# A post-norm decoder on one core: the row of maxima sent from ScalarE's DMA queue, and new due times for two phases

## The reference, cut to what matters

```python
# layer 0; layer 1 is the same without the bias, its q, k and v go through a width of 64
q, k, v = heads(x @ Wq), heads(x @ Wk), heads(x @ Wv)          # (16, 16 heads, 512, 16)
logits = einsum('bhqd,bhkd->bhqk', q, k) / 4 + fourier_bias     # bias(h, i - j)
attn = softmax(where(causal, logits, -inf))
x = layernorm(x + einsum('bhqk,bhkd->bhqd', attn, v) @ Wo)
# layer 0 goes on: cross-attention to 64 context rows, then ten gated experts of width 128 (top 2 of 8, 2 shared)
# layer 1 goes on: cross-attention to the same context, then a feed-forward of width 1024 with a sine in it
```

## Time and profile before

| | us |
|---|---|
| median of 3 runs (lowest, highest) | 4129.87 (4127.6, 4133.61) |
| the profiled execution: its own time | 4140.3 |
| its span from first to last instruction | 4138.5 |
| phase 1: first piece to last | 64 to 1540 |
| phase 2 | 1577 to 3359 |
| phase 3 | 3370 to 4138 |

### The profile page before, as it was taken

One profiled execution on the slowest core, in us unless ns is written; L12 is line 12 of the kernel. 1 busy time (PEld: TensorE's weight loads), 2 busy tenths in 40 slices (PEclk: granted clock), 3 DMA queues, 4 the chain that ended last, 5 costly groups with the idle time before them and its releaser, 6 DMA issues. The chain is left out here.

```text
span 4138.5 us, 59033 instructions
## 1 busy us (share of the span) xinstructions
PE 3415.8 (83%) x19630; PEld 2589.5 (63%) x19630; DVE 2920.1 (71%) x8450; ACT 1999.0 (48%) x3687; POOL 1285.3 (31%) x1713
## 2 busy tenths in 40 slices
PE   3888898888888845799999999999998756888886
PEld 2566666666666534567777777777776535666664
DVE  5578787777787743566666666766665436999996
ACT  3455555555555522244444444444444334666564
POOL 1134333343333431122222222222222102444443
PEclk8899999899999967999999999999999767999998
DMA  7444434444344112244444444444443320000000
GB/s 180 73 83 74 79 70 95 78 79 76 69 98 74 26 36 65 59 74 84 83 83 83 83 83 83 85 85 84 83 86 69 70 74 1 27 25 31 21 26 16
DMA packets 207788, 284.55 MB, mean 69 GB/s; under 512 B 50880, under 2 KB 136128, under 8 KB 198784
## 3 DMA queue, kind: packets, MB, share of 16 engines
q1 hardware_dynamic: 207488, 280.78, 34.1%
HBM read 179.75 MB, written 96.73 MB: 67 GB/s over the span
## 5 line engine op out<-in xcount | busy, mean ns | idle before, releaser
L1308 DVE CUSTOM_DVE_ANT_0 ps<-ps,future 128x512 f32<-128x512 f32 (+3 forms) x2048 | 958.0, 513 | 337.1 <-PE ps L942 330.0
L1629 ACT ACTIVATE pt<-ps 128x512 f32<-128x512 f32 x1280 | 720.3, 597 | 512.8 <-PE ps L963 499.8
L963 PE MATMUL ps<-q_stack,k_stack 97*128 97x512 f32 (+3 forms) x2048 | 566.5, 356 | 211.0 <-DMA q_stack<-nmaxT 179.0
L1812 POOL TENSOR_SCALAR_AFFINE_SELECT pt<-pt 128x256 f32<-128x256 f32 x1024 | 401.1, 429 | 738.0 <-ACT pt L1629 737.6
L942 PE MATMUL ps<-k_stack,q_stack 96*128 96x512 f32 (+3 forms) x2048 | 543.5, 350 | 52.8 <-DVE nmax L1308 33.6
L963 PEld LDWEIGHTS ps<-q_stack,k_stack 97*128 97x128 f32 x2048 | 367.4, 200 | 349.0 <-DMA q_stack<-nmaxT 212.2
L942 PEld LDWEIGHTS ps<-k_stack,q_stack 96*128 96x128 f32 x2048 | 378.1, 205 | 130.2 <-issue 44.2
L1834 POOL TENSOR_TENSOR hid<-hid,gate_of 128x512 f32<-128x512 f32 x128 | 164.3, 1283 | 690.7 <-DVE hid L1448 690.7
L977 PE MATMUL ps<-pt,v_ones 128*32 128x512 f32 (+3 forms) x4096 | 335.1, 472 | 31.9 <-POOL pt L1812 31.8
L816 PE MATMUL ps<-eh,w_hi 128*128 128x512 f32 (+1 forms) x672 | 281.5, 419 | 13.9 <-DVE xl L1289 11.4
L1308 DVE DVE_READ_ACCUMULATOR2_ANT nmax<- 128x1 f32 x2048 | 285.7, 139 | 0.3
(11 more groups left out here) (272 smaller groups left out, 8122.7 us busy)
## 6 DMA issues: line engine op xcount, KB each, us to landing
qk_scratch<-parts SPq DMA_DIRECT2D x64, 1024.0 KB, 5.8
q_stack<-qk_scratch SPq DMA_DIRECT2D x384, 128.0 KB, 5.0
k_stack<-qk_scratch SPq DMA_DIRECT2D x384, 128.0 KB, 5.7
gate_of<-gate_scratch SPq DMA_DIRECT2D x128, 256.0 KB, 5.0
x_mid<-x_ring SPq DMA_DIRECT2D x32, 512.0 KB, 2.6
x_ring<-x_mid SPq DMA_DIRECT2D x32, 512.0 KB, 5.1
w_stage<-in_w SPq DMA_DIRECT2D x17, 512.0 KB, 10.4
x_ring<-in_x SPq DMA_DIRECT2D x16, 512.0 KB, 4.6
```

The lines of the kernel that those rows point to most:

```text
L963: done = e.matmul(bank(bank_of[piece])[:, at:at + SEQ - j * P], a.k[0:97, base + h, j * P:(j + 1) * P], a.q[0:97, base + h, j * P:SEQ], st ...
L1308: done = e.tensor_tensor_reduce(src, src, future[:, SEQ - width:SEQ], -1.0, 3e38, ALU.add, ALU.min, nmax[:, g % 2, u // 5 * 2 + h, t:t + 1])
L1629: e.activation(dst, src, ACT.Exp).then_inc(exp_up.sem)
L1812: done = e.affine_select(out=blk, in_=blk, compare_op=ALU.is_ge, fill=0.0, base=0, pattern=[[0, 2], [1, P]], channel_multiplier=-1)
```

## The change

`mr` moves from SyncE's program to ScalarE's, with the same wait and the same DMA, and the due times of phases 1 and 2 are all new. Phase 3 is untouched. The numbers of pieces stay the same.

```diff
 TABLE = {
-    1: (74.24, {
+    1: (74.79, {
         "tensor": {
...
-            "N": [10.33, 35.92, 49.97, 68.22],
-            "PV": [39.6, 50.95, 65.92, 80.92],
+            "N": [25.914, 49.331, 63.644, 80.459],
+            "PV": [54.077, 65.337, 76.55, 94.888],
...
-            "xv": [95.77],
+            "xv": [103.921],
...
         "scalar": {
...
-            "N": [10.68, 36.36, 50.32, 68.96],
+            "N": [26.78, 49.641, 63.913, 80.701],
+            "mr": [27.324, 51.039, 64.237, 81.053],
...
         "sync": {
-            "ld 1": [-78.68],
-            "send": [-42.19, -34.21],
-            "rows": [-37.05, -26.06, -11.85, 4.41],
-            "mr": [16.55, 36.73, 51.02, 69.33],
-            "st 1": [183.02],
-            "kl": [81.48],
+            "ld 1": [-84.38],
+            "send": [-25.748, -17.605],
+            "rows": [-22.895, -13.151, 1.014, 47.474],
+            "st 1": [205.092],
+            "kl": [91.368],
         },
     }),
-    2: (91.43, {
+    2: (91.03, {
...
         "scalar": {
...
+            "mr": [138.692, 161.135, 182.14, 202.403],
...
         "sync": {
...
-            "mr": [128.05, 152.69, 182.69, 201.54],
...
-        max_row = [signal(f"max_row{k}", "sync", "mr", 1, 16, lambda key, k=k: key[1] % 2 == k) for k in range(2)]
+        max_row = [signal(f"max_row{k}", "scalar", "mr", 1, 16, lambda key, k=k: key[1] % 2 == k) for k in range(2)]
...
@@ in scalar(e) @@
+                elif kind == "mr":
+                    n, g = key
+                    a = att[n // BATCH]
+                    base = (g % a.sets) * GROUP
+                    e.wait_ge(*nmax_copy[key])
+                    e.dma_start(a.q[96:97, base:base + GROUP, :].bitcast(F32).rearrange("p h (t q) -> p (h t) q", q=P),
+                                a.nmaxT[:, :].bitcast(F32)).then_inc(max_row[g % 2].sem, 16)
@@ in sync(e) @@
-                elif kind == "mr":
...
```

More of the change, by code:

```diff
@@ L127 @@
 TABLE = {
-    1: (74.24, {
+    1: (74.79, {
         "tensor": {
[21 rows of a table removed]
[23 rows of a table added]
         },
         "scalar": {
[16 rows of a table removed]
[18 rows of a table added]
         },
         "vector": {
[17 rows of a table removed]
[18 rows of a table added]
         },
         "gpsimd": {
[L190 to L195, removed]
+            "sel": [45.796, 52.932, 61.307, 63.867, 73.059, 75.047, 89.481, 93.418],
+            "ln a0": [114.094],
+            "tb x0": [122.81],
+            "xs": [135.171, 140.315, 146.923, 151.897, 158.674, 161.06, 167.095, 170.965],
+            "xe": [141.859, 143.757, 153.041, 158.142, 162.556, 165.821, 173.869, 174.921],
+            "ln x0": [194.141],
@@ L207 @@
         "tensor": {
[25 rows of a table removed]
[25 rows of a table added]
         },
         "scalar": {
[19 rows of a table removed]
[20 rows of a table added]
         },
         "vector": {
[18 rows of a table removed]
[18 rows of a table added]
         },
         "gpsimd": {
-            "tb a1": [54.64],
-            "sel": [143.18, 148.25, 164.75, 172.21, 191.62, 196.65, 209.64, 216.88],
-            "ln a1": [269.21],
-            "h2": [None, None, -37.99, -29.93, -19.31, -11.84, 0.07, 7.56, 16.45, 22.74],
-            "ln ex": [42.94],
+            "tb a1": [123.318],
+            "sel": [172.319, 185.37, 202.259, 207.051, 228.077, 232.025, 243.304, 250.411],
@@ L281 @@
+            "ln a1": [305.965],
+            "h2": [None, None, -2.365, 7.429, 15.398, 21.908, 35.083, 41.236, 50.486, 56.541],
+            "ln ex": [76.515],
         },
         "sync": {
-            "ld 2": [-87.57],
-            "send": [74.31, 94.78],
-            "rows": [104.53, 124.28, 146.7, 170.94],
-            "mr": [128.05, 152.69, 182.69, 201.54],
-            "st 2": [273.18],
-            "gh": [-48.24],
-            "sg": [-46.41, -45.9, -36.67, -28.61, -17.99, -9.09, 1.38, 8.88],
+            "ld 2": [-38.115],
@@ L290 @@
+            "send": [109.08, 138.923],
+            "rows": [141.11, 160.207, 187.217, 210.043],
+            "st 2": [307.51],
+            "gh": [-18.786],
+            "sg": [-9.841, -6.46, -0.9, 5.922, 18.591, 28.003, 36.64, 43.797],
         },
@@ L1940, in sync @@
                                             "(h d) t -> d h t", d=HDIM)).then_inc(rows_in[g % a.sets].sem, 16)
-                elif kind == "mr":
-                    n, g = key
-                    a = att[n // BATCH]
-                    base = (g % a.sets) * GROUP
-                    e.wait_ge(*nmax_copy[key])
-                    e.dma_start(a.q[96:97, base:base + GROUP, :].bitcast(F32).rearrange("p h (t q) -> p (h t) q", q=P),
-                                a.nmaxT[:, :].bitcast(F32)).then_inc(max_row[g % 2].sem, 16)
                 elif kind == "kl":
```

## The result

| | before | after |
|---|---|---|
| median of 4 runs (lowest, highest), us | 4130.17 (4127.6, 4133.61) | 4034.82 (4020.1, 4036.3) |
| ratio after / before, 95% interval | | 0.9761 [0.9737, 0.9785] |
| profiled execution: own time, span, us | 4140.3, 4138.5 | 4036.08, 4034.3 |
| phase 1, phase 2, phase 3, us | 1478.5, 1784.4, 768 | 1412.1, 1745.6, 769 |

The changed kernel is 95 us faster at the median. 180 were forecast. The time lies inside the range, which had been drawn wide enough to take in rival A, and the gain is more than twice that of rival A (36 us).

A forecast was written before the change was run, and what follows sets the result against it. TensorE was taken as the bound in phases 1 and 2, its longest wait being T's for the row of maxima. -150 - 65 + 30 + 5 = -180 us gave 3960 profiled, 3950 us at the median; range 3850 to 4095.

The forecast's parts named there:

- rival A: Landing of the row of maxima stays as long as before despite ScalarE's queue: -36 us, 4094 us; chance 0.13.
- the short landing: On ScalarE's queue a row of maxima lands in 1.8 to 2.5 us, with nothing ahead in its ring.
- Part 3: New order in phases 1 and 2: less cover costs 1.9 us a batch in phase 1, 0 in phase 2; +30 us.
- Part 1: `mr` on ScalarE's queue: 85% of T's 179 us wait for the row of maxima won, -150 us.
- Part 2: TensorE's clock partly recovers as idle time goes: 2 us a batch in phase 1, 2.1 in phase 2; -65 us.
- (a): Phase 1: xv waits for kl, 0 to 2 us, taken as 1 us.
- (b): PV.1 to PV.3 have 1.2 to 1.9 us behind the last T; PV.3 loses 0.4 of its cover.
- (c): xq.0 has 2.0 us of cover behind tc x0, before 5.5; wait of 0 to 1.5 us, taken as 0.7.
- shifts that I can't see: Unseen effects of the new order, taken as a loss of 0.8 us.
- (d): A batch of phase 1 runs some 10 us longer in the table, counted once when the last batch drains: +5 us.
- C: T.0.0 of phase 1 waits for a late mr.0 amid kl and rows.3: slower, 4213 or 4161 us; chance 0.09.
- B: VectorE or GpSimd takes over in phase 1, which gains nothing: about -80 us, 4050 us; chance 0.11.

The follow-up runs named there:

- run 4: Changed kernel with two of the six DMAs of each `rows` group, 256 KB instead of 768, all engines doing the same work: 3848.38 us, ratio 0.9296.
- run 3: Changed kernel with SyncE holding back rows.3 and rows.1 in phase 1 and rows.2 in phase 2 until a row of maxima has landed: 4010.13 us, 0.9681.
- run 8: Kernel before with two due times changed, so SyncE issues mr.2 and mr.3 of phase 1 ahead of the `rows` they followed: 4049.76 us, 0.9777.
- run 2: Kernel before, old due times, with only `mr` moved to ScalarE's program right behind each N: 4121.19 us, 0.9957.
- run 5: Changed kernel with SyncE holding back rows.3 and rows.1 until mr.0 and mr.2 have landed, in phase 1 only: 3970.25 us, 0.959.
- run 6: Run 5 plus 15 due times of phase 2 that put more work ahead of T.1.0 and T.3.0: 3918.35 us, 0.9461.
- run 10: Kernel before with the changed kernel's due times for xs, xe, xp and xo of phase 1, moved 13.54 us earlier: ratio 1.0106.
- run 7: Kernel before with xe.1, xe.3 and xe.5 put ahead of the next xs on VectorE and GpSimd: 4165.6 us, 1.0055.
- run 9: Kernel before with xs.4 to xs.7 of phase 1 put on TensorE ahead of the xp they follow: ratio 1.0102.

## Why the prediction was right or wrong, point by point

**What bounds the kernel: right.** TensorE's idle time and above all the wait of T for the row of maxima was the thing to win; run 4 took it away and phase 2 was left with 1.3 us of idle time a batch.

**The cause of the long landing: right in the bytes, wrong in the queue.** I had read that the long ones are those behind `rows`, and wrote "the bytes ahead in the ring". Runs 3, 4 and 8 show that it is the transfers under way at the issue; run 2 and the change itself show that the ring doesn't matter. The step that failed is "I take the short landing, since its own ring has nothing ahead of it": not 1.8 to 2.5 us but 3.9 at the median over all 128, and 6.7 for the group of the example, since the row of maxima lands behind all that SyncE issued before it (121 of 121 times). The Trainium skill (DMA: Bandwidth & Descriptors, Issuing engines are not separate DMA queues) says that a second issuer only saves issue time. The traces agree: mr.1 of phase 2 lands in 6.9 us from SyncE's queue and in 6.7 from ScalarE's. I had set it against the rule of turns by packets (same page, Queues, rings and completion order) and sided with that one, which the landings here don't bear out.

**The number: inside the range by luck.** The range reached up to 4095 to take in rival A, the case in which the forecast's mechanism is wrong, and that case came. Of the signs that I had named for being right, T's wait (133.9 us, not below 40), the landing (3.9, not 1.8 to 3), the batches (82.5 and 100.6, not 78 to 80 and 95 to 97), the clock of phase 1 (0.93, not 0.95) and the wait of xv (none, not 1 us) all failed; the clock of phase 2 (0.99) and the length of phase 3 (769) held. Part 3, booked as a cost of 35 us, was a gain of some 45 and made up for part of what Part 1 missed.

**Part 1, -150 us forecast.** T's waits fell by 45 us, of which the queue alone brings 16 (run 2). The rest is cover that the new order puts in front of T.1.0 in phase 2, and in phase 1 T.2.0, whose row leaves earlier and which comes 5.9 us behind N.2 and not 4.6. I had added up 3.5 there; 1.3 of the 5.9 are waits of S.3.1 and PV.1 (0.6 before), which hide the landing and win nothing. T.3.0 of phase 2 lost 1.6 us by the change, its row landing in 5.2 us and not 3.8. No run shows a cost on ScalarE, which I took at 0.

**Part 2, the clock, -65 us forecast.** It hung on Part 1. TensorE's busy time fell by 0.4 and 0.7 us a batch, 16 x 1.1 = 18 us. In phase 2 the clock rose from 0.97 to 0.99, nearly what I had taken, but TensorE was busy for 0.7 us a batch less and not 2.1. In phase 1 it stayed at 0.93. The price was right in size where the wait went: 1.4 us of time for each microsecond of T's wait in run 8, 1.7 in run 4. It is no constant: from run 5 to run 6 a batch of phase 2 lost 5.1 us of T's wait and 4.5 us of its length, since other waits came.

**Part 3, the new order, +30 us forecast: wrong in sign.** Apart from T's waits, TensorE's idle time fell by 1.3 us a batch in phase 1 where I had 1.9 more. (a) No wait of xv for `kl`: 0 and not 1. (b) PV.1 to PV.3 wait 1.4 us a batch more and not 0.4 (2.7 for 1.3), each of them 0.4 to 0.5 more, while I had given a loss to PV.3 alone. (c) No wait of xq.0: 0 and not 0.7. The score banks gave 1.1 (I had 1): S and N wait 0.3 us a batch for VectorE and not 2.1, but S now waits 0.7 for the bank that the copy of N leaves. The "shifts that I can't see", at +0.8, were a gain of 1.6. I had looked for places with less cover and hardly for those with more.

**Part 3 (d), the drain, +5 forecast: -24.** I read a later end in the table as a later end in time. In the drain due times aren't kept; what counts is the order within the block (11 us, run 10) and something ahead of it that stays open.

**The rivals.** A had the mechanism: landings stay. Its time, 4094, was 59 us too high through the two errors of Part 3, worth some 80 us together, and in phase 1 through T.2.0, for which I carried a landing of 6.4 us and over although mr.2 lands in 4.7. Against these, phase 2 waits 5.1 us a batch and not 3.3, mostly at T.3.0. C happened in part: T.0.0 of phase 1 waits 2.6 us, beyond the 1.3 from which C was to decide the sign (2.3, had I kept the 15 us of clock that A counts), mr.0 landing 5.6 us after its issue amid `kl` and rows.3. It didn't turn the sign because it was the only wait left there: T.2.0 and T.3.0 wait 0.4 us together and not 4.3. B did not happen: with the landing short, phase 1 takes 77 to 79 us a batch (runs 3 to 6 and 8), VectorE busy for 66 or 67 of them. The sum of the whole is then, by spans: batches of phase 1 -44 us, its drain -24, batches of phase 2 -29, start and end of phase 2 -10, the rest +2: -104 in the profiled executions, -95 at the medians.

## What to carry to other kernels

A small DMA that an engine waits for must be issued ahead of the big ones, or they behind it; giving it a queue of its own didn't get it past the transfers that were already under way. Where TensorE was the bound, taking such a wait away gave 1.4 to 1.7 us of the whole time for each microsecond of it, since the clock came back with it. And a hand-balanced order is one thing: moving one block of it (runs 7, 9, 10) cost half a per cent to one per cent each time, though each looked like a gain by itself; in two of the three the idle time stayed as it was and the clock fell, so a list of waits alone doesn't show the loss.

## What the runs showed of the hardware

An 8 KB DMA alone in its queue took 1.8 us to land with nothing else moving and 6.4 to 7.6 us when 768 KB had been issued in another queue in the 3 us before. The trace's packets show where the time goes: quiet, its first data packet starts 1.2 us after the issue; in phase 2 behind rows.2 it starts 3.7 us after it, the last semaphore packet comes at 5.4, and the landing is at 6.7, while 730 KB move in SyncE's queue. Quiet, the last packet ends at 1.4 and the landing is at 1.8. So the late start is only half of it; the packets are spread out too, and the landing comes later behind the last of them. In mr.0 of phase 1 that last part is the largest: packets from 2.3 to 3.8 us behind the issue, landed at 5.6. In all cases the landing is behind that of every DMA issued before, whichever of the two queues it is in (121 of 121 here, 123 of 123 in run 2). Issued 0.6 us ahead of the same 768 KB in one and the same queue, it takes 1.8 us (run 8): it isn't held up by what comes 0.6 us behind it. Whether it is a shared path to memory, the engines themselves or the descriptors' own handling that holds it up was not told apart.
